# Extra multiplies of a tile of ones on TensorE in the prologue of an attention and expert-mixture kernel

## What is computed

```
h  = layernorm(x)                                  # over the 512 positions
q, k, v = split(h^T @ w_in^T + b_in)               # 8 heads of 16 channels
s  = q k^T / sqrt(16), only where |i - j| <= 64    # a band of 128 positions
o  = softmax(s) v @ w_out^T + b_out
x  = x + (relu(o^T) * ctx) mixed over channels by w_ct + b_ct
h2 = layernorm(x)                                  # 2048 rows of 512
x  = x + routed(h2) + shared(h2)                   # top 2 of 16 experts, and one shared expert
```

## Time and profile before

| what | us |
|---|---|
| median of 3 runs | 720.66 |
| lowest and highest | 717.82 and 722.0 |
| the profiled execution | 721.22 |
| its span | 719.0 |
| TensorE busy | 660.6 (92%) |
| VectorE busy | 390.9 (54%) |
| GpSimd busy | 427.8 (60%) |
| mean granted clock | 0.966 |

### The profile page before, as it was taken

How to read it: one execution, slowest core, us unless ns; L and a number is a source line. 1 busy time by engine, 2 the same in 40 slices (tenths; PEclk the granted TensorE clock), 3 DMA queues, 4 the chain that set the end, 5 groups by cost and what they waited for, 6 DMA issues and landing times.

```text
span 719.0 us, 14013 instructions
## 1 busy us (share of the span) xinstructions
PE 660.6 (92%) x4134; PEld 323.6 (45%) x4134; DVE 390.9 (54%) x1424; ACT 367.1 (51%) x689; POOL 427.8 (60%) x653
## 2 busy tenths in 40 slices
PE   3679899999999999988999999899999989999992
PEld 1345455555555555544445545333333333333330
DVE  3789888888888888851124786322222222222220
ACT  4248667777777767656323222344444344444441
POOL 5248788888888887766110001137767567758763
PEclk8579999999999999999899999999999999999997
DMA  6544544554554433212495943434665566544530
GB/s 211 158 120 114 143 123 130 152 138 133 137 137 137 114 108 102 76 31 79 146 405 189 421 156 120 146 81 99 108 139 128 122 134 123 113 105 83 88 50 0
DMA packets 65275, 95.25 MB, mean 132 GB/s; under 512 B 18345, under 2 KB 43049, under 8 KB 63145
## 3 DMA queue, kind: packets, MB, share of 16 engines
q1 hardware_dynamic: 50544, 66.49, 30.2%
q0 software_dynamic: 9600, 18.89, 14.8%
q10 hardware_dynamic: 5058, 8.99, 3.7%
HBM read 50.99 MB, written 19.14 MB: 98 GB/s over the span
## 4 chain that ended last, share of the span: by engine, by line
PE 67%; DVE 13%; issue 7%; POOL 5%; DMA 4%; ACT 1%; SPq 1%; POOLq 0%; ACTq 0%; DVEq 0%
PE bank L774 18%; PE bank L805 8%; DVE bank L1171 7%; PE bank L600 5%; PE bank L761 4%; PE bank L565 4%; PE bank L793 4%; PE bank L651 4%; PE bank L583 3%; PE bank L754 3%; PE bank L739 3%; PE bank L785 2%; PE bank L659 2%; PE bank L620 2%; PE bank L672 2%
## 5 line engine op out<-in xcount | busy, mean ns | idle before, releaser
L1171 DVE CUSTOM_DVE_ANT_0 bank<-bank,cb 128x192 f32<-128x192 f32 (+1 forms) x512 | 186.0, 418 | 32.8 <-PE bank L565 32.5
L942 ACT ACTIVATE wgu<-bank 128x384 f32<-128x384 f32 (+1 forms) x256 | 125.6, 547 | 45.9 <-PE bank L583 45.4
L774 PE MATMUL bank<-wgu,rowsT 128*64 x320 | 145.9, 599 | 0.0
L776 PE MATMUL bank<-X,rowsT 128*64 128x512 f32 x320 | 145.9, 598 | 0.0
L1404 DVE TENSOR_TENSOR act_in<-act_in,bank 128x256 f32<-128x256 f32 x56 | 23.6, 421 | 201.1 <-ACT act_in L1061 175.7
L565 PE MATMUL bank<-wgu 96*128 96x192 bf16 (+1 forms) x512 | 95.0, 271 | 20.2 <-DVE wgu L1171 14.5
L456 POOL TENSOR_SCALAR_AFFINE_SELECT wgu<-wgu 128x512 f32<-128x512 f32 (+1 forms) x128 | 74.5, 582 | 47.2 <-ACT wgu L942 46.9
L499 POOL DMA_INDIRECT rows<-xn_rows,gather_i x40 | 44.4, 1109 | 88.6 <-DVE gate_of L1399 61.8
L517 POOL DMA_INDIRECT out<-y_out,scatter_i x40 | 65.5, 1638 | 30.6 <-issue 23.0
L517 POOL DMA_INDIRECT out<-y_out,scatter x40 | 58.5, 1462 | 42.0 <-DMA out<-y_out,scatter_i 25.6
L565 PEld LDWEIGHTS bank<-wgu 96*128 96x128 bf16 x512 | 45.2, 101 | 79.9 <-DVE wgu L1171 39.3
(11 more groups left out here) (174 smaller groups left out, 1116.0 us busy)
## 6 DMA issues: line engine op xcount, KB each, us to landing
wgu<-wgu SPq DMA_DIRECT2D x190, 128.0 KB, 2.5
wgu<-w_gu SPq DMA_DIRECT2D x16, 1024.0 KB, 13.1
X<-w_d SPq DMA_DIRECT2D x16, 512.0 KB
out<-y_out ACTq DMA_DIRECT2D x17, 256.0 KB, 3.3
X<-x SPq DMA_DIRECT2D x16, 256.0 KB, 3.3
wgu<-ctx SPq DMA_DIRECT2D x16, 256.0 KB, 3.2
xn_rows<-xn SPq DMA_DIRECT2D x16, 256.0 KB, 2.4
rows<-xn_rows ACTq DMA_DIRECT2D x16, 256.0 KB, 3.5
```

Of the source, the lines that this page charges most:

```text
L774: mm(gb[k.buf][0:GROUP, :], rowsT[:, k.buf, c, 0:GROUP], wgu[:, bass.ds(e * 2048 + 512 * c, 512)], start=(c == 0), stop=(c == 3))
L776: last = mm(gb[k.buf][GROUP:P, :], rowsT[:, k.buf, c, GROUP:P], gu_half[:, k.buf, 512 * c:512 * c + 512], start=(c == 0), stop=(c == 3))
L942: nc.scalar.activation(probs[j % 4][:, 2 * half:2 * half + 2, 0:w], s2[half][:].rearrange("p (j c) -> p j c", j=2)[:, :, 0:w], ACT.Exp, sc ...
L1171: last = v.tensor_tensor_reduce(o, o, cb[:, B_MASK + off:B_MASK + off + w], 1.0, MASKED * 2.0, ALU.add, ALU.max, rowmaxes[n % 2][:, h + i, ...
```

## The change

TensorE multiplies `ones_f` by itself, 128 columns in float32, into the first bank of `s2`, and nobody reads the result. It does so 13 times before anything else (as soon as `ones_f` is set, ahead of its waits for weights and constants), 14 times behind the second `project_q`, and in eight units of the first two sequences' scores twice between the halves and once behind them. DVE sets `ones_f` before the other tiles. In all that is 13 + 14 + 8 x 3 = 51 multiplies.

```diff
+ALONE = (0, 2, 4, 5, 6, 8, 9, 10)
...
+            def keep_busy(times):
+                for _ in range(times):
+                    mm(s2[0][:, 0:P], ones_f[:], ones_f[:], start=True, stop=True)
+
+            pe.wait_ge(setup, 1)
+            keep_busy(13)
             pe.wait_ge(weights_in, 16)
-
             pe.wait_ge(consts_in, 16)
...
                 if p := piece(U, -1):
                     scores(*p, 0)
+                    if U in ALONE:
+                        keep_busy(2)
                 if p := piece(U, 11):
                     shifted_scores(*p, 0)
                     shifted_scores(*p, 1)
                 if p := piece(U, -1):
                     scores(*p, 1)
+                    if U in ALONE:
+                        keep_busy(1)
...
                     project_q(n)
+                    if n == 1:
+                        keep_busy(14)
...
             v = nc.vector
+            v.memset(ones_f[:], 1.0).then_inc(setup, 1)
             for b in range(3):
                 v.memset(vaug[b][:, :, :, D:2 * D], 1.0).then_inc(setup, 1)
-            v.memset(ones_f[:], 1.0).then_inc(setup, 1)
             v.memset(y_out[:, 1, :], 0.0).then_inc(setup, 1)
```

## The result

The changed kernel takes 728.46 us (median of 6 runs, 726.94 to 730.25), against 720.76 for the kernel before on the same chip. The ratio is 1.0111, with a 95% interval of 1.0086 to 1.0136. By the medians the change makes the kernel 7.7 us slower. I had forecast 715.3 and a range of 712.8 to 719.2; what came is rival C, to which I gave 8% and 726.7.

A forecast was written before the change was run, and what follows sets the result against it. The low clock in the first 45 us, making VectorE wait for scores, was taken as the bound; 0 + 0 - 6.0 + 0.1 = -5.9 us brings the execution from 721.22 to 715.3, range 712.8 to 719.2.

The forecast's parts named there:

- rival C: In the scores: the new 16-row multiplies don't raise the clock, PE's path stays at 0.50; 726.7 us, chance 8%.
- What bounds the kernel: First 45 us: at the low clock VectorE waits for the scores, seven waits, 6.2 us together.
- The price of one new multiply: On TensorE, one new multiply costs 0.43 us at clock 0.50, 0.23 at 1.00; upper end 0.76, lower 0.21.
- Part 1: 13 multiplies ahead of the first q, with the earlier `ones_f`: worth 0 (0 to +3.6 us).
- Part 2: 14 multiplies behind the second q: cost 0 (0 to +1.3 us), and the first scores find the clock at 1.00.
- Part 3: Scores at clock 1.00: VectorE's waits of 6.2 us go, less 0.2; gain given as 5.9 us.
- Part 4: 24 multiplies among the scores: cost 0.1 us (0 to 0.5); at clock 0.50 each of eight units loses about 0.7.
- Rival A: Cold stretches of 19.08 to 31.30 and 34.80 to 44.95 halve: gain 11.2 us, time 710.0, chance 3%.
- rival B: Among the scores the clock rises but drops once more; 3 to 4 us of gain go, 717.5 to 719; 14%.

The follow-up runs named there:

- the kernel with the blocks alone: The changed kernel (16 rows) with only the 13 and the 14 multiplies, none among the scores: 718.85 us, ratio 0.9986 to the kernel before.

## Why the prediction was wrong

*What bounds the kernel* was right: the clock up to 45 us, and VectorE's waits for the scores as the measure of what it costs. With 128 rows VectorE's waits up to 60 us went from 6.5 us in eight to 1.1 in four, and the time from the first scores to the mark from 47.33 us to 41.60 and 41.48. That is 5.7 and 5.9 us of gain where my sum has 5.9. The ratios 0.9891 and 0.9916, 7.9 and 6.0 us, hold the noise of the later stages besides.

*The price of one new multiply* was right for a stream of them: 0.43 by the row of `project_v`, 0.44 to 0.45 measured. The upper end of 0.76 wasn't needed.

*Part 1* was right in its 0: the first q began at 7.13 instead of 6.90, but the second at 12.51 against 12.50, and the kernel with the blocks alone has a ratio of 0.9986. One detail was wrong: the clock was not up for the first q, which took 2.04 us.

*Part 2 is the step that failed.* I wrote that "such a stream keeps PE wholly busy" and compared this with the busy 10.36 of 12.22 us before the clock rose at 31.30. The busy share counts a multiply of 16 rows like one of 128, and the clock doesn't. In the changed kernel TensorE was wholly busy for 44.8 us, from 13.56 to 58.40, and the clock was 0.50 from 14 to 58. The row on which I rested the argument is made of multiplies of 96 and 128 rows, and no row of the kernel before shows a stream of 16. I used `project_v` for the duration and took it for the effect on the clock too, without bounding that from below. By itself the part cost little (0.60 us in the changed kernel, 0.08 with the blocks alone, inside my 0 to 1.3); what failed is the clock that it was to hand to the scores.

*Part 3* fell with it, since the clock was never up; in the kernel with 128 rows it is as I worked it out. *Part 4* had the right fallback in words, "a unit costs PE 1.95 against 1.26", but was too low: 2.73, as I left out the 0.2 us at each of four changes. Rival C, whose mechanism is what happened, adds 5.5 us with that price, and the mark came 11.8 late. Eight units of 0.77 are 6.2 us, about what it lacks; but it also leaves out the 3.5 us at 1.00 that the kernel before has from 31.30 on, and how the rest divides was not taken apart. That its 726.7 is still near the median of 728.46 is in part luck. Its 8% were too few: the doubt that it names, 16 of 128 rows, had nothing in the trace against it. What I held against it, that other streams held the clock up later, was again said of high multiplies.

In the same way the 80% of busy time by which I held that the clock stays was no evidence. With 128 rows the share is 78% (16.55 of 21.20) and the clock stays; with 16 it is 100% and the clock doesn't rise.

*Rival A*, half of the whole cold stretch or 11.2 us, did not come in the kernels that did raise the clock: 5.7 and 5.9 us up to the mark, with VectorE busy 20.38 of 21.20 us. It is what the rule of "TensorE: Matmul & The Clock Gate" in the Trainium skill (Terms) gives; these traces do not agree with it as a measure of what can be won here.

Some sums of the prediction are slightly off, and nothing hangs on them. The gain of part 3 is 6.2 - 0.2 = 6.0, as the last sum has it, and not 5.9. TensorE's work at the high clock is (10.36 + 7.61) / 2 + 1.28 = 10.3, not 10.4. And rival B with 3 to 4 us given back is 718.3 to 719.3, not 717.5 to 719.

## What to carry to other kernels

To hold TensorE's clock up with filler work, give it the full 128 rows: at the low clock a multiply takes as long (0.43 us with 128 rows, 0.44 with 16), and by the ratios 16, 32 and 64 rows cost 4 to 8 us here where 128 gained 6 to 8. All filler here was 128 columns in float32; other widths and heights between 64 and 128 were not tried. Filler that doesn't raise the clock is worse than none, since it runs at the low clock on the path; so look first at the granted clock behind a block of it, not at the busy share. And put it where the clock is lost, between the short multiplies that wait for another engine: 24 there gave 3.3 us up to the mark, 27 ahead of them 1.1, and all 51 together 5.7 to 5.9, as the ones ahead have the clock up at the first scores and the others keep it. Last, measure a change in a prologue at a mark just behind it: the span of one profile moved by 2.7 us with a shift of 0.1 at the mark.

## What the runs showed of the hardware that I had not expected

- A stream of 28 records of 16 rows, 100% busy for 6.1 us, did not raise the clock, which fell to 0.50 in its first 0.5 us. The same stream with 128 rows raised it (4.04 us behind a second q at the low clock). With 64 rows it didn't.
- Behind a stream of 26 such records at the start the first q took 1.10 us with 128 rows, and 2.04 to 2.05 with 16, 32 and 64.
- Zeros times zeros hold the clock as well as ones times ones (41.99 and 41.77 us up to the mark, ratios 0.9937 and 0.9926).
- A switch between float32 multiplies of ones and bfloat16 scores costs some 0.2 us at the low clock, four of them 0.77 in one unit.
- The granted clock of 1.00 at a trace's start can be a blank: multiplies there took as long as at 0.50 (2.04 us for q against 1.12).
